# A decoder layer's self-attention loop: queries taken by VectorE, copies in front of projections, split forget-gate columns

## The reference

```python
xn = layer_norm(x, in_ln_w, in_ln_b)
q, k, v, p, y = split(xn @ W_in.T + b_in)         # 512, 512, 512, 512, 16 columns
k = (1 - smear) * k + smear * k_prev              # the key one position before
pos = cumsum(sigmoid(y))                          # forget gates, one per head
scores = (q/s) @ (k/s).T / sqrt(32) + causal - (pos[i] - pos[j])
out = (silu(p) * (softmax(scores) @ v)) @ W_out.T
x1 = layernorm(x + layer_norm(out, out_ln_w, out_ln_b))
```

## Time and profile before

| | us |
|---|---|
| median of 3 runs | 2677.26 |
| profiled execution | 2674.3 |
| its span, first to last instruction | 2672.5 |
| TensorE busy | 2363.7 (88%) |
| VectorE busy | 1866.2 (70%) |
| ScalarE busy | 1760.6 (66%) |
| GpSimd busy | 1033.2 (39%) |

### The profile page before, as it was taken

How to read it: one execution, slowest core, us unless ns; L and a number is a source line. 1 busy time by engine, 2 the same in 40 slices (tenths; PEclk the granted TensorE clock), 3 DMA queues, 4 the chain that set the end, 5 groups by cost and what they waited for, 6 DMA issues and landing times. The chain is left out here.

```text
span 2672.5 us, 62026 instructions
## 1 busy us (share of the span) xinstructions
PE 2363.7 (88%) x18020; PEld 1960.6 (73%) x18020; DVE 1866.2 (70%) x5239; ACT 1760.6 (66%) x4480; POOL 1033.2 (39%) x1112
## 2 busy tenths in 40 slices
PE   5888888886799999999999999999999379999991
PEld 4676777674577777777777777777776279999990
DVE  5666766666577766876677666776686368788776
ACT  4888888885466666666566666766576256676662
POOL 3453444444443333333333334333332134444434
PEclk8999999999899999999999999999999689999995
DMA  4645554453100000000000000000000166777765
GB/s 126 175 109 116 126 130 107 111 120 80 33 10 16 17 17 1 16 17 17 3 15 16 17 9 8 16 17 17 1 16 9 65 221 226 242 235 229 240 220 197
DMA packets 160230, 224.40 MB, mean 84 GB/s; under 512 B 33873, under 2 KB 127697, under 8 KB 159569
## 3 DMA queue, kind: packets, MB, share of 16 engines
q1 hardware_dynamic: 149040, 201.88, 26.9%
q0 software_dynamic: 9664, 20.53, 2.3%
q10 hardware_dynamic: 1376, 0.54, 0.1%
HBM read 140.15 MB, written 24.01 MB: 61 GB/s over the span
## 5 line engine op out<-in xcount | busy, mean ns | idle before, releaser
L1358 ACT COPY x_pt<-x_ptb 128x512 f32<-128x512 f32 x512 | 272.2, 583 | 193.6 <-PE x_ptb L1800 192.9
L1553 DVE CUSTOM_DVE_ANT_0 wox<-x_score,x_mask_add 128x512 f32<-128x512 f32 x352 | 239.3, 683 | 166.5 <-PE x_score L1788 115.3
L1352 ACT ACTIVATE wox<-wox,x_low 128x512 f32<-128x512 f32 x352 | 251.8, 718 | 100.8 <-DVE x_low L1553 97.4
L1254 POOL TENSOR_TENSOR x_k_lo<-x_whole,x_k_hi 128x512 fp32r<-128x512 f32 x128 | 164.5, 1285 | 336.8 <-ACT x_k_hi L1399 335.1
L484 ACT ACTIVATE prob<-prob,low 128x128 f32<-128x128 f32 (+1 forms) x512 | 233.7, 468 | 55.3 <-DVE low L727 54.0
L1817 PE MATMUL x_av<-x_pt,x_vx 128*64 128x256 f32 x2048 | 249.3, 385 | 0.6 <-ACT x_ox_hi L1366 0.6
L1532 DVE COPY x_whole<-x_proj 128x512 f32<-128x512 f32 x192 | 130.6, 686 | 128.4 <-PE x_proj L1718 127.1
L1564 DVE TENSOR_SCALAR wox<-wox,x_rden 128x512 f32<-128x512 f32 x352 | 201.9, 615 | 0.6
L2217 ACT ACTIVATE h_t<-h_bank,b_s 128x256 f32<-128x256 f32 x312 | 130.8, 470 | 107.2 <-PE h_bank L2436 99.7
L2436 PE MATMUL h_bank<-xg_hi,w_hi 128*128 128x256 f32 x624 | 177.9, 285 | 22.1 <-DVE xg_lo L2309 20.7
L1817 PEld LDWEIGHTS x_av<-x_pt,x_vx 128*64 128x64 f32 x2048 | 135.5, 136 | 80.8 <-issue 11.8
(11 more groups left out here) (296 smaller groups left out, 8080.0 us busy)
## 6 DMA issues: line engine op xcount, KB each, us to landing
w_s<-w SPq DMA_DIRECT2D x156, 512.0 KB, 4.9
k_parts<-k_hi SPq DMA_DIRECT2D x128, 128.0 KB, 2.4
q_parts<-q_hi SPq DMA_DIRECT2D x128, 128.0 KB, 2.4
k_parts<-pos_parts SPq DMA_DIRECT2D x128, 64.0 KB, 2.4
k_parts<-k_lo SPq DMA_DIRECT2D x64, 128.0 KB, 2.4
q_parts<-q_lo SPq DMA_DIRECT2D x64, 128.0 KB, 2.4
w_s<-expert_rows SPq DMA_DIRECT2D x16, 512.0 KB, 5.0
b_s<-b SPq DMA_DIRECT2D x39, 128.0 KB, 3.0
```

Source lines behind the costliest of these rows:

```text
L1254: pool.tensor_tensor(part_of(n, q_lo, k_lo), whole_of(n), part_of(n, q_hi, k_hi).bitcast(F32), ALU.subtract).then_inc(low_ready.sem, 1)
L1352: nc.scalar.activation(slot, slot, ACT.Exp, bias=low[:, u:u + 1], scale=-1.0, accum_out=den[:, u:u + 1]).then_inc(exp_ready.sem, 1)
L1358: nc.scalar.copy(pt[:, u % PX_RING, :], ptb[u % 2][:, :]).then_inc(pt_taken[u % 2].sem, 1)
L1553: dve.tensor_tensor_reduce(prob_slot(u), score[u % 2][:, :], mask_add[:, :], -X_SCALE, 3.0e38, ALU.add, ALU.min, low[:, u:u + 1]).then_inc ...
```

## The change

Six things are done, all in `self_phase`:

1. **Queries.** VectorE takes q from the bank (`take_q`, four `tensor_scalar` in steps 8 and 9), ScalarE only makes the high part from it (`high_q`, one cast of 128x512 in steps 9 and 10).
2. **Copies in front.** In each of ScalarE's steps `take_transposed` stands ahead of the projection parts.
3. **Forget gates.** y's weights (`win_y`) are split into a high and a low part and y is done in six matmuls, in step 3 in front of k's first chunk, behind the wait on `xn_split`; `take_y` moves from ScalarE's step 3 to 4.
4. **VectorE's table.** `forget_gates` moves from step 4 to 6, `centred` from 6 to 7, `place_pos` from 9 to 10, silu from 8 to 11, `residual_sum` from 11 to 12, `residual_stats` from 12 to 15, and in step 14 the gate stands ahead of `half_p`. The next row's statistics stay in step 10.
5. **Start.** One cast and one subtraction for y's weights.
6. **GpSimd** waits for `q_hi_ready` in front of `q_lo`.

```diff
-        win_y = sb("win_y", [P, KC, W_COLS - 4 * D_EXP])
+        win_y = sb("win_y", [P, KC, HEADS])
+        win_y_hi = sb("win_y_hi", [P, KC, HEADS], F32R)
+        win_y_lo = sb("win_y_lo", [P, KC, HEADS], F32R)
...
@@ gpsimd, low_q
-                    f = QP + n
-                    pool.wait_ge(proj_taken[f % 2].sem, proj_taken[f % 2].at(b, f // 2 + 1))
+                    pool.wait_ge(q_hi_ready.sem, q_hi_ready.at(b, n + 1))
...
@@ scalar
+            nc.scalar.copy(win_y_hi[:], win_y[:]).then_inc(consts_a, 1)
...
-            def take_q(b, n, i):
+            def high_q(b, n):
                 f = QP + n
-                if n == 0 and i == 0:
+                if n == 0:
                     act.wait_ge(q_split.sem, q_split.at(b - 1, 2))
-                filled(b, f)
-                m = 2 * n + i
-                for dst in (q_t, q_hi):
-                    ins = nc.scalar.activation(dst[:, m, :], proj[f % 2][:, i * S:(i + 1) * S], ACT.Identity,
-                                               bias=q_bias[:, m:m + 1], scale=q_scale[:, m:m + 1])
-                if i == 1:
-                    taken(ins, f)
+                act.wait_ge(proj_taken[f % 2].sem, proj_taken[f % 2].at(b, f // 2 + 1))
+                nc.scalar.copy(q_hi[:, 2 * n:2 * n + 2, :], q_t[:, 2 * n:2 * n + 2, :]).then_inc(q_hi_ready.sem, 1)
...
-            steps = {1: [take_xt], 3: [take_y], 4: [lambda b: smear_k(b, 0)], 5: [lambda b: smear_k(b, 1)], 6: [lambda b: high_k(b, 0)],
-                     7: [lambda b: high_k(b, 1), lambda b: take_q(b, 0, 0)], 8: [lambda b: take_q(b, 0, 1)], 9: [lambda b: take_q(b, 1, 0)],
-                     10: [lambda b: take_q(b, 1, 1), take_output(0)], 11: [take_output(1)], 13: [lambda b: tanh_p(b, 0)],
-                     14: [lambda b: tanh_p(b, 1)]}
+            steps = {1: [take_xt], 4: [take_y, lambda b: smear_k(b, 0)], 5: [lambda b: smear_k(b, 1)], 6: [lambda b: high_k(b, 0)],
+                     7: [lambda b: high_k(b, 1)], 9: [lambda b: high_q(b, 0)], 10: [lambda b: high_q(b, 1), take_output(0)],
+                     11: [take_output(1)], 13: [lambda b: tanh_p(b, 0)], 14: [lambda b: tanh_p(b, 1)]}
...
                     exps(b, i)
+                    take_transposed(*unit(b, i - COPY_LAG))
                     for part in parts.get(i, ()):
                         part(b)
-                    take_transposed(*unit(b, i - COPY_LAG))
...
@@ vector
+            dve.tensor_tensor(win_y_lo[:], win_y[:], win_y_hi[:].bitcast(F32), ALU.subtract).then_inc(consts_v, 1)
...
+            def take_q(b, n):
+                f = QP + n
+                if n == 0:
+                    dve.wait_ge(q_split.sem, q_split.at(b - 1, 2))
+                filled(b, f)
+                for i in range(2):
+                    m = 2 * n + i
+                    ins = dve.tensor_scalar(q_t[:, m, :], proj[f % 2][:, i * S:(i + 1) * S],
+                                            q_scale[:, m:m + 1], q_bias[:, m:m + 1], ALU.mult, ALU.add)
+                taken(ins, f)
...
-                     8: [lambda b: one_over_sums(b, 1), silu],
...
+                     8: [lambda b: one_over_sums(b, 1), lambda b: take_q(b, 0)],
+                     9: [lambda b: widen(b, 1), lambda b: take_q(b, 1)],
+                     10: [place_pos, lambda b: x_stats(b + 1)],
+                     11: [silu],
...
@@ tensor
-                in_sbuf(b, XT)
-                full(project(bk_[0:HEADS, 0:S], lambda k: win_y[:, k, :], lambda k: xn_t[:, k, :], KC))
+                pe.wait_ge(xn_split.sem, xn_split.at(b, 1))
+                full(project_parts(bk_[0:HEADS, 0:S], lambda a, k: (win_y_hi, win_y_lo)[a][:, k, :],
+                                   lambda a, k: xn_parts[a][:, k, :]))
...
-            split_parts = {3: [k_chunks[0]], 4: k_chunks[1:3], 5: k_chunks[3:], 6: q_chunks[0:2], 7: q_chunks[2:3], 8: q_chunks[3:],
+            split_parts = {3: [inputs[1], k_chunks[0]], 4: k_chunks[1:3], 5: k_chunks[3:], 6: q_chunks[0:2], 7: q_chunks[2:3], 8: q_chunks[3:],
...
-            whole_parts = {0: inputs[:1], 2: inputs[1:2], 9: outputs[:1], 10: outputs[1:]}
+            whole_parts = {0: inputs[:1], 9: outputs[:1], 10: outputs[1:]}
```

More of the change, by code:

```diff
@@ L229, in self_phase @@
         pos_steps, p_half_ready = sig("pos_steps", 4), sig("p_half_ready", 2)
+        q_hi_ready = sig("q_hi_ready", 2)
         q_split, k_split = sig("q_split", 2), sig("k_split", 2)
@@ L241, in self_phase @@
         av_done, gated = sig("av_done", HPC), sig("gated", HPC)
-        N_CONSTS, N_VCONSTS, N_IN, N_LATE = 10, 8 + KC, 16 * (9 + 2 * EC), 16 * 4
+        N_CONSTS, N_VCONSTS, N_IN, N_LATE = 10, 9 + KC, 16 * (9 + 2 * EC), 16 * 4
         xn_hi_ready, xn_split = sig("xn_hi_ready", 1), sig("xn_split", 1)
@@ L557, in projections @@
                 for n in range(2):
-                    for i in range(2):
-                        take_q(b, n, i)
+                    high_q(b, n)
                 for n in range(2):
@@ L634, in _ @@
                                   ALU.subtract).then_inc(consts_v, 1)
+            dve.wait_ge(consts_a, 2 + KC + 1)
+            dve.tensor_tensor(win_y_lo[:], win_y[:], win_y_hi[:].bitcast(F32), ALU.subtract).then_inc(consts_v, 1)
             for s in (x1_stored, score_taken):
@@ L774, in _ @@
             for n in range(2):
+                take_q(-1, n)
+            for n in range(2):
                 half_p(-1, n)
@@ L780, in _ @@
                      3: [lambda b: out_stats(b - 1)],
-                     4: [lambda b: one_over_sums(b, 0), forget_gates],
+                     4: [lambda b: one_over_sums(b, 0)],
                      5: [lambda b: widen(b, 0), lambda b: gate(b - 1, 3)],
-                     6: [lambda b: take_k(b, 0), lambda b: centred(b - 1)],
-                     7: [lambda b: take_k(b, 1)],
-                     8: [lambda b: one_over_sums(b, 1), silu],
[L786 to L789, removed]
-                     13: [lambda b: widen(b, 2), lambda b: half_p(b, 0)],
-                     14: [lambda b: half_p(b, 1), lambda b: gate(b, 0)],
-                     15: [lambda b: gate(b, 1)]}
-            last = {**steps, 4: steps[4][:1], 6: steps[6][1:], 7: [], 9: steps[9][:1], 10: [], 13: steps[13][:1], 14: steps[14][1:]}
+                     6: [lambda b: take_k(b, 0), forget_gates],
+                     7: [lambda b: take_k(b, 1), lambda b: centred(b - 1)],
+                     8: [lambda b: one_over_sums(b, 1), lambda b: take_q(b, 0)],
+                     9: [lambda b: widen(b, 1), lambda b: take_q(b, 1)],
+                     10: [place_pos, lambda b: x_stats(b + 1)],
+                     11: [silu],
+                     12: [lambda b: one_over_sums(b, 2), lambda b: residual_sum(b - 1)],
+                     13: [lambda b: widen(b, 2), lambda b: half_p(b, 0)],
+                     14: [lambda b: gate(b, 0), lambda b: half_p(b, 1)],
+                     15: [lambda b: gate(b, 1), lambda b: residual_stats(b - 1)]}
+            last = {**steps, 6: [], 7: steps[7][1:], 10: [], 14: steps[14][:1]}
+            for i in (8, 9, 13):
+                last[i] = steps[i][:1]
             def one_pass(b, parts):
@@ L859, in project_y @@
                 bk_ = free(b, YP)
-                in_sbuf(b, XT)
-                full(project(bk_[0:HEADS, 0:S], lambda k: win_y[:, k, :], lambda k: xn_t[:, k, :], KC))
+                pe.wait_ge(xn_split.sem, xn_split.at(b, 1))
+                full(project_parts(bk_[0:HEADS, 0:S], lambda a, k: (win_y_hi, win_y_lo)[a][:, k, :],
+                                   lambda a, k: xn_parts[a][:, k, :]))
             def chunk(b, f, i, col0):
                 bk_ = free(b, f) if i == 0 else proj[f % 2]
-                if f == KP and i == 0:
-                    pe.wait_ge(xn_split.sem, xn_split.at(b, 1))
                 ins = project_parts(bk_[:, i * S:(i + 1) * S], lambda a, k: win_parts[a][:, k, col0:col0 + P],
```

## The result

The changed kernel takes 2649.33 us, median of 4 runs (2647.79 to 2650.51), against 2677.11 for the kernel before on the same chip. The ratio is 0.9889 with a 95% interval of 0.9874 to 0.9904: faster by 27.8 us, where 38.7 were forecast. The profiled execution has a span of 2648.7 against 2672.5.

A forecast was written before the change was run, and what follows sets the result against it. TensorE, 86% busy in the self-attention loop, was taken as the bound, with waits mainly on ScalarE and clock drops. 15 x 33.95 + 12 x 1.5 = 527.3 against 567, start +1: 2635.6 us profiled, median 2638.6, range 2615 to 2663.

The forecast's parts named there:

- A pass: Self-attention loop, one pass without a clock drop: 36.30 + 0.3 - 2.65 = 33.95 us.
- copies in front and y split together: Steps 1 to 3: the idle stretch is moved behind transposes and scores, not removed; +0.3 us per pass.
- queries -2.65: Steps 7 to 10: moving queries to VectorE removes two TensorE waits with their slow restarts, 1.3 and 1.35 us per pass.
- The wait for `q_hi`: Step 10, output 1: TensorE's wait of 1.2 us goes, 1.35 with as slow a restart.
- the restart in step 9: Step 9: TensorE's wait of 1.16 us for `pt` and its slow restart go, 1.3 us together.
- rival B: VectorE comes late in steps 6, 7, 10, 11, 14, 15; half of 2.65 given back, 2658 us; chance 0.18.
- C: GpSimd runs x1 before `xn_lo`: y and k wait 3.8 us more per pass, 2696; cover 2.4; chance 0.05.
- D: No change: TensorE's stalls return elsewhere in full, as the loop's ring had its own period; chance 0.04.
- Drops: Falls of TensorE's clock to 1.2 GHz after idle time near a pass's start: 12 of 1.5 us, about 13 before.
- Rival A: Clock stays up because work splits the idle stretch: 15 x 33.95 = 509.3, 18 us less, 2620; chance 0.11.
- Ends: Start and end of the loop: y after `xn_lo`, one more cast and subtraction, later x1; +1 us, bounds -1 and +3.
- The forecast's side sentence: Steps 11 to 15: moving silu gives `k_lo` 0.65 us back, taken from `q_lo` or `zx`; sum the same unless cover is used up.

The follow-up runs named there:

- the kernels with the copies behind: Changed kernel with ScalarE's copies again behind the projection's instructions: 2637.6 us with y split; 2637.2 us with y's product also back in step 2 with whole weights.
- y whole: Changed kernel with y's product back in step 2, four matmuls with whole weights on xn_t: 2622.4 us.
- useless matmuls: Changed kernel with four more matmuls before TensorE's wait for xn_lo, their result overwritten by the split product: 2630.42 us, ratio to before 0.9819.

## Why the prediction was right, and by what it missed

- **A pass.** 33.95 forecast without a drop, 33.87 measured. Its parts: copies in front and y split together +0.3, measured 33.87 - 33.52 = +0.35; queries -2.65, measured -2.8. The wait for `q_hi` went, the restart in step 9 too. VectorE's busy time grew by 2.5 a pass and not by 1.7; silu, 0.7 longer, is the difference. Of rival B only a trace came (the wait for `k_t` grew from 5.8 to 8.5 in all), of C and D nothing. The row of `xn_lo` in GpSimd's order shows rival C's margin, 2.4 forecast and 2.17 there:

```profile
374.01 2.44 POOL L414 TENSOR_SCALAR x<-res,mv,rstd 128x256 f32<-128x256 f32 x2 [0.20 <-issue]
378.62 1.27 POOL L399 TENSOR_TENSOR xn_lo<-xn_t,xn_hi 128x512 fp32r<-128x512 f32 x1 [2.17 <-ACT xn_hi L502]
```

- **Drops.** 12 of 1.5 in 15 passes forecast; in the thirteen passes, 10 stretches that cost (456.0 - 13 x 33.87) / 10 = 1.57. By the forecast the thirteen passes come to 13 x 33.95 + 10.4 x 1.5 = 457.0; they were 456.0. The count was a guess from the idle time in all, and in part lucky: the kernels with the copies behind have one stretch of 2.2 and 7 and 9 stretches, and here three passes have two each. Rival A (the clock stays up) was wrong for this kernel, since y stood behind the same wait. For y whole its clock was right, and that its 2620 lies 2 us from 2622.4 is luck: a pass there takes 33.25 and not 33.95, and the first pass and the later phases, which A had no loss in, make up for it.
- **First pass: the mis-sized term.** Every pass was given -2.65; this one came out at +2.4, 5 us off. The working costed SyncE's queue in the steady loop only. The late-weight loads stand ahead of pass 0's load alone, and the wait of VectorE for it, 6.36 us, was in the profile of before. With the load in front the changed kernel's first pass is 7.0 shorter.
- **Ends.** +1 forecast for start and end. Start -0.7 and the lone last pass with its tail +2.0 make +1.3; the last preparing pass is 1.6 short of its -2.65. Together they are 2 us worse than forecast; no run was made on them.
- **Later phases: a term that was not there.** "Not touched" was read as "not changed". They cost +7.2, of which 5.1 are the cross-attention rows and VectorE's code.
- **The sum.** First pass 5.1, the thirteen passes 0.9 (they gave 33.6 and not 13 x 2.65 = 34.5, since before they took 37.66 each and not 37.8), ends 1.9, later phases 7.2: 15.1 short, against 38.7 - 23.8 = 14.9; the rest is rounding. By the medians the miss is 10.9, as the profiled execution of before lies 3 under its median and that of the changed kernel 1.2 over. The number was in range although 12 us of the miss lie outside what the working replayed.
- **GpSimd beside VectorE.** The forecast's side sentence had moving silu give `k_lo` its 0.65 us back; it did not. Silu itself takes 1.91 where it took 1.21, and GpSimd's tiny `var_eps` beside it 1.19 in place of 0.23. But `k_lo` has `centred`, another instruction with two SBUF inputs, beside it now:

```profile
355.25 3.27 POOL L389 TENSOR_TENSOR k_lo<-k_t,k_hi 128x512 fp32r<-128x512 f32 x2 [3.45 <-ACT k_hi L530]
360.94 1.47 POOL L382 TENSOR_TENSOR q_lo<-q_t,q_hi 128x512 fp32r<-128x512 f32 x1 [2.42 <-ACT q_hi L513]
...
363.96 1.19 POOL L373 TENSOR_SCALAR var_eps<-mv 128x2 f32<-128x2 f32 x1
```

The Trainium skill, GPSIMD Engine Reference, section 1 Specifications, says that GpSimd shares its SBUF interfaces with VectorE and contends with such instructions. The trace agrees: both sides slow down, and the cost goes where the neighbour goes. No run moved silu alone, so that it is the neighbour and nothing else is read from the order of time, not tested.

## What to carry to other kernels

Ask of each idle stretch of TensorE how long it is in one piece, and what stands close to it: here cutting an idle stretch of 2.0 to 2.3 us into pieces of 0.8 and less earned 16 to 18 us over the loop, even with useless matmuls, while putting y's product behind the longest wait lost what the cut had gained. Replay the first pass by itself, with the loads that stand only in front of it. When phases that an edit does not touch change their time, pad the engine whose "issue" time grew by a few instructions before looking for a cause in the edit.

## What the runs showed of the hardware

- TensorE's clock: in the kernel before, an idle stretch of 2.27 in each pass went with 1.2 GHz in 11 of 13 passes; 0.70 and 2.04, with 1.0 of work between them, in 7 of 13, and three of these for 6.8 us on end (such a pass costs 3.3 us more, one with a single stretch mostly 1.25 to 1.5); 0.70, 0.42, 0.59 and later a single 1.85, in none; 0.70 and 0.81, in none.
- Six or twelve more instructions in VectorE's program cost 0.2 and 0.35 us a row in a loop that begins some 650 us later; eighteen cost nothing.
- Silu, one VectorE instruction on 128x1024, takes 1.21 us in the kernel before and 1.91 in the changed one, hardly differing from pass to pass (a mean of 1.210 over 13 and 1.906 over 13).
